# Power in two parts at six layer norms, one power for a double normalisation, and combination weights stacked on 72 partitions in two mixture routers

## The chip, the cores and the metric

One NeuronCore of a Trainium2 chip runs the whole program; the other seven are idle. The metric is device time of one execution in microseconds (us), lower is better. The program is one launch: everything from the inputs in HBM to the output in HBM lies inside it.

## The reference, cut to what matters

A graph network of four layers on 625 nodes with 512 features and 10,000 edges. Each layer adds a graph part and a feed-forward part to the residual `x`, and each part begins with a layer norm over the 512 features of a node:

```
x = x + L0_gnn(layernorm(x));  x = x + L0_ffn(layernorm(x))   # SAGE; causal attention, then softmax mixture of 8 experts
x = x + L1_gnn(layernorm(x));  x = x + L1_ffn(layernorm(x))   # 2 graph-transformer layers; top-2 experts
x = x + L2_gnn(layernorm(x));  x = x + L2_ffn(layernorm(x))   # EGC convolution; 8 experts with top-2 weights
x = x + L3_gnn(layernorm(x));  x = x + L3_ffn(layernorm(x))   # GCN convolution; top-2 experts
```

`layernorm(x) = (x - mean) / sqrt(var + 1e-5)`. `L0_ffn` itself starts with a layer norm of its own, so two normalisations follow each other there. Its mixture, and that of `L2_ffn`, compute every expert for every node and weigh the results:

```
out = sum_e comb[:, e] * (gelu(x @ W1[e] + b1[e]) @ W2[e] + b2[e])
```

with `comb` the softmax of the router's logits (in `L2_ffn` zeroed outside the two largest).

## The kernel before, in words

**Layout.** The residual `X` lies in SBUF as 5 tiles (T) of 125 nodes on 125 partitions (R), 512 features along each. Matmuls contract over features, so a normalised tile set `XN` is transposed by TensorE (PE) in 128x125 pieces into PSUM (L760, `ln_to_feats`) and copied to `XT`, 4 chunks (C) of 128 features by 625 nodes; VectorE (DVE) copies three of the tiles (L1911), ScalarE (ACT) two (L1473). Products that need accuracy are made of two `fp32r` parts, a rounded high part and a low remainder: DVE subtracts to get the lows.

**Order.** Nothing is scheduled by a tool. Each engine has its instruction list written by hand (the five blocks `sync`, `gpsimd`, `tensor`, `scalar`, `vector`), and the lists meet at counting semaphores. `Chain` counts an engine's own operations on a semaphore, and `c.sync()` lets the engine wait for its own last one. `keep(b, n)` (L771) issues n matmuls on constants into a free PSUM bank where PE would otherwise have nothing to do.

**Layer norms.** `ln0` to `ln8` are one pattern: five row statistics (L1922, one per tile), five aggregations to mean and variance (L1930), one small operation `ve = var + eps` on all five columns (L1932), a power of -0.5 on GpSimd (POOL) by `power()` (L641, `rstd`), then five normalisations on DVE (L1958). `ln1` is written out: its statistics alternate with the additions that make `X` (L1996), and it runs the pattern twice on the 5 numbers per node (power, L2458, L2460, L2462, power again as `ln(2)`, L2465) and then normalises once (L2468). At the same time PE and ACT build the causal graph masks (L1266; ACT L1761 and L1764), and PE's transposes of `ln1` wait for these masks too.

**Mixture routers** (r = 0 in layer 0, r = 2 in layer 2). DVE makes `COMB` (125 nodes x 5 tiles x 8 experts; L2062, L2081). PE transposes it to 8 x 625 (L962). ACT copies it as plain fp32 `combT` (L1534) and as rounded high part `combH` (L1540), DVE subtracts to `combL` (L2093). Both halves lie in 128 partition tiles that ACT had zeroed. PE then spreads the weights of each expert over 128 partitions by matmuls with a selector, in halves of 375 and 250 nodes (`HALVES`), high and low (L977, L978):

```
g = 2 * e + i
if g >= 3:
    pe.wait_ge(S("rt_cb"), 2 * E * (r // 2) + g - 2)
pe.matmul(bank[:, (7, 3, 4)[g % 3], 0:n], SEL[:, e], spreadH[:, lo:lo + n], start=True, stop=False)
```

and ACT copies all 16 pieces to `CB` (L1545) from three banks in turn. Before the spread PE runs `soft_first(r, 0)` and `(r, 1)`, the first products of two units (a unit is one expert and one half; 12 matmuls each, L948). `open_sums` (L955) puts `comb . b2` into the five output banks, one fp32 matmul of K=8 each, three of them inside the spread, two in the mixture. The mixture runs over 16 units: PE `soft_first`, ACT gelu (L1563; its first one loads an activation table), DVE times `CB` (L2315), ACT rounding (L1571), DVE low part (L2321), PE `second` (L997).

**GpSimd and SyncE.** POOL's list starts with constants (L598 on). SP issues the loads; `b2` is loaded on 8 partitions.

Of the kernel before, what the change touches and what calls it, by code (L numbers as in the profile page):

```python
# [113 lines left out]
def graph_network(nc, A, out):  # L114
    ctx = ExitStack()
    with ctx:
# [141 lines left out]
        spreadH, spreadL = (rounded("rB", at, N + 1) for at in (0, 632))  # L258
        combH, combL = (x[0:E, 0:N] for x in (spreadH, spreadL))
# [173 lines left out]
        NORMS = 6 + 2 * T + 2 * LAYERS  # L433
        POW = {"ln0": 1, "degr": 2, "bn0": 3, "ln1": 4, "ln2": 5, "q": 6, "k": 6 + T, "ln3": 6 + 2 * T, "lf": NORMS + 1, "ln4": NORMS + 2,
               "ln5": NORMS + 3, "l2": NORMS + 4, "ln6": NORMS + 5, "ln7": NORMS + 6, "bn3": NORMS + 7, "ln8": NORMS + 8}
        LN = [0, 12] + [16 * (k - 1) for k in range(2, 9)]
        RT_ACT = {0: 0, 1: 9, 2: 14, 3: 23}
# [2334 lines left out]
```

## Time and profile before

| | us |
|---|---|
| median of 3 runs | 1692.26 (1690.21 to 1693.14) |
| the profiled execution's own time | 1694.99 |
| span of that profile | 1693.2 |
| PE busy | 1610.8 (95%), 8735 instructions |
| DVE busy | 1231.3 (73%), 2095 |
| ACT busy | 939.7 (55%), 1590 |
| POOL busy | 283.4 (17%), 262 |

Busy times are of the one profiled execution. PE's share contains the filler matmuls of `keep` and stretches in which it ran at half clock, so it isn't the share of useful work. An instruction line of the trace gives its start, its duration (of a group of neighbours: of the whole group, with "xN"), the engine and line, output<-input with partitions x elements, and in brackets the engine's idle time before it and what ended that.

### The profile page before, as it was taken

How to read it: one execution, taken by the hardware profiler on the slowest of the kernel's cores; microseconds unless marked ns; L12 is line 12 of the kernel's file. 1: busy time of each engine (PE TensorE's matmuls, PEld its weight loads, DVE VectorE, ACT ScalarE, POOL GpSimd, SP SyncE). 2: the span in 40 equal slices, each digit the busy share in tenths (PEclk: the TensorE clock that was granted, in tenths of full speed). 3: DMA queues.
4: the chain of work that ended last, by engine and by line, in shares of the span. 5: the costliest groups of instructions: out<-in, count | busy, mean ns of one | idle time of the engine just before them, and what ended most of it. 6: DMA issues, size and time to landing. Idle time of an engine off the chain costs nothing. (4 is left out here: it accounts for less than half of the span.)

```text
span 1693.2 us, 26308 instructions
## 1 busy us (share of the span) xinstructions
PE 1610.8 (95%) x8735; PEld 1252.0 (74%) x8735; DVE 1231.3 (73%) x2095; ACT 939.7 (55%) x1590; POOL 283.4 (17%) x262
## 2 busy tenths in 40 slices
PE   9998999999989998889999999999899999999998
PEld 8886766868866886468778765775588888888886
DVE  8837661464755574779999768353599999999997
ACT  1424464443623462149999653431288788877884
POOL 0014530010210121069000301000280000000003
PEclk9998999999999999989999999999999999999999
DMA  8010000022000002044853240005043529936003
GB/s 335 14 51 1 1 2 13 1 113 75 2 26 13 1 2 100 25 144 160 323 197 106 80 162 0 1 1 223 25 161 145 234 73 384 364 151 242 21 22 97
DMA packets 42176, 173.09 MB, mean 102 GB/s; under 512 B 10187, under 2 KB 10440, under 8 KB 26617
## 3 DMA queue, kind: packets, MB, share of 16 engines
q1 hardware_dynamic: 28678, 153.68, 23.8%
q0 software_dynamic: 8960, 10.29, 2.3%
q10 hardware_dynamic: 4464, 8.13, 1.3%
q8 instruction: 47, 0.77, 0.2%
q14 instruction: 27, 0.22, 0.0%
HBM read 275.47 MB, written 19.25 MB: 174 GB/s over the span
## 5 line engine op out<-in xcount | busy, mean ns | idle before, releaser
L695 POOL DMA_INDIRECT sb_W<-slots_out,sb_slus x20 | 31.5, 1574 | 545.4 <-DMA slots_out<-sb_rC 539.9
L1489 ACT ACTIVATE sb_rF<-sb_rF,sb_nmx 125x625 f32<-125x625 f32 (+4 forms) x120 | 89.5, 746 | 45.0 <-DVE sb_nmx L2011 44.9
L771 PE MATMUL bank<-sb_ones 128*128 128x512 f32 x220 | 102.9, 617 | 8.8 <-DVE sb_rC L2558 6.3
L641 POOL TENSOR_TENSOR sb_rstd<-sb_ve,sb_half 125x5 f32<-125x5 f32 (+1 forms) x17 | 19.1, 1123 | 478.0 <-DVE sb_ve L1932 267.0
L381 DVE TENSOR_TENSOR sb_rA_r<-sb_W,sb_rA_r 128x1024 fp32r<-128x1024 f32 x68 | 83.2, 1224 | 12.2 <-ACT sb_rA_r L1588 12.0
L2011 DVE CUSTOM_DVE_ANT_0 sb_rF<-bank,sb_rG 125x625 f32<-125x625 f32 x80 | 61.5, 807 | 36.1 <-PE bank L863 35.2
L771 PEld LDWEIGHTS bank<-sb_ones 128*128 128x128 f32 x220 | 41.9, 196 | 57.8 <-issue 48.7
L381 DVE TENSOR_TENSOR sb_XT_r<-sb_W,sb_XT_r 128x1024 fp32r<-128x1024 f32 x68 | 83.3, 1225 | 0.0
L381 DVE TENSOR_TENSOR sb_rB_r<-sb_W,sb_rB_r 128x1024 fp32r<-128x1024 f32 x68 | 83.0, 1221 | 0.0
L1588 ACT ACTIVATE sb_rA_r<-sb_W 128x1024 fp32r<-128x1024 f32 x68 | 71.5, 1052 | 20.0 <-DMA sb_W<-in_w_m 15.9
L1623 ACT ACTIVATE sb_rG_r<-bank 128x512 fp32r<-128x512 f32 x51 | 30.6, 600 | 82.3 <-PE bank L1075 82.3
L903 PE MATMUL bank<-sb_rA,sb_rDE 125*64 125x125 f32 x1040 | 69.3, 276 | 4.5 <-DVE sb_rA L2025 4.3
L2315 DVE TENSOR_TENSOR sb_rF<-sb_rF,sb_rDE 128x375 f32<-128x375 f32 (+1 forms) x32 | 15.4, 486 | 79.7 <-ACT sb_rF L1563 79.7
L875 PE MATMUL bank<-sb_ident,sb_rF 125*125 125x125 f32 x520 | 70.1, 279 | 3.0 <-DVE sb_nmx L2011 3.0
L1588 ACT ACTIVATE sb_XT_r<-sb_W 128x1024 fp32r<-128x1024 f32 x68 | 71.7, 1054 | 0.0
L1588 ACT ACTIVATE sb_rG_r<-sb_W 128x1024 fp32r<-128x1024 f32 x68 | 71.6, 1053 | 0.0
L1588 ACT ACTIVATE sb_rB_r<-sb_W 128x1024 fp32r<-128x1024 f32 x68 | 71.3, 1049 | 0.2 <-PE bank L1053 0.2
L903 PEld LDWEIGHTS bank<-sb_rA,sb_rDE 125*64 125x64 f32 x1040 | 54.9, 136 | 20.7 <-DVE sb_rA L2025 13.1
L875 PEld LDWEIGHTS bank<-sb_ident,sb_rF 125*125 125x125 f32 x520 | 61.5, 189 | 9.0 <-issue 6.8
L381 DVE TENSOR_TENSOR sb_AT_r<-sb_W,sb_rG_r 128x1024 fp32r<-128x1024 f32 x51 | 62.0, 1216 | 0.0
L2025 DVE COPY sb_rA<-bank 125x500 f32<-125x500 f32 (+3 forms) x60 | 37.6, 627 | 31.0 <-PE bank L875 30.9
L1049 PE MATMUL bank<-sb_XT_r,sb_rC_r 128*128 128x512 f32 x136 | 59.4, 437 | 0.0
(534 smaller groups left out, 4839.1 us busy)
## 6 DMA issues: line engine op xcount, KB each, us to landing
sb_W<-in_w_m SPq DMA_DIRECT2D x204, 1024.0 KB
sb_rDE<-in_w_m SPq DMA_DIRECT2D x17, 1024.0 KB
sb_rC<-slots_in SPq DMA_DIRECT2D x33, 256.0 KB, 2.7
sb_W<-in_w_g SPq DMA_DIRECT2D x8, 1024.0 KB, 4.9
slots_out<-sb_rC ACTq DMA_DIRECT2D x31, 256.0 KB, 2.0
slots_in<-sb_rC SPq DMA_DIRECT2D x1, 4608.0 KB, 24.7
sb_W<-in_w_a SPq DMA_DIRECT2D x4, 1024.0 KB, 17.9
sb_W<-in_w_m SPq DMA_DIRECT2D x2, 2048.0 KB, 16.4
```

The lines of the kernel that those rows point to most:

```text
L381: eng.tensor_tensor(lo, src[:, HALF * h:HALF * (h + 1)], hi.bitcast(F32), ALU.subtract).then_inc(split(r, p, h, b, "lo")[0], 1)
L641: pool.tensor_tensor(dst, src, half8[0:src.shape[0], :].broadcast_to([src.shape[0], k]), ALU.pow).then_inc(S("pow"), 1)
L695: pool.indirect_dma_start(out=G[r][k][:, t], out_offset=None, in_=YS[0:P * KEPT[r]], in_offset=bass.IndirectOffsetOnAxis(ap=slus[:, k, t:t ...
L771: pe.matmul(bank[:, b, :], ones[:], ones[:, 0:1].broadcast_to([P, D]), start=True, stop=True)
L875: return pe.transpose(bank[0:R, b, at:at + R], SM[:, (2 * p + a) % 4, kb * R:(kb + 1) * R], ident[0:R, 0:R])
L903: mm = pe.matmul(bank[a * DH:(a + 1) * DH, 6 + g % 2, p % 2 * R:(p % 2 + 1) * R], V[:, kb, h + a, :], PT[:, p % 2, 8 + a if kb == 4 else 4 ...
L1049: pe.matmul(dst, high[2 * h + k], w_hi[:, k], start=(opens and h == 0 and k == 0), stop=False)
L1489: act.activation(SM[:, s % 4, 0:kn], SM[:, s % 4, 0:kn], ACT.Exp, scale=-1.0, bias=nmx[:, s:s + 1], accum_out=dens[:, s:s + 1]).then_inc(S ...
L1588: act.activation(half(r, p, h)[0], part(PLACE[r][p])[:, HALF * h:HALF * (h + 1)], ACT.Copy).then_inc(split(r, p, h, b, "hi")[0], 1)
L1623: act.activation(hTh[:, j % 2], src, ACT.Copy).then_inc(S("b_ht"), 1)
L2011: dve.tensor_tensor_reduce(out=SM[:, s % 4, 0:kn], in0=scores, in1=mask(t), scale=-1.0, scalar=3e38, op0=ALU.add, op1=ALU.min, accum_out=n ...
L2025: dve.tensor_copy(PT[:, p % 2, 4:4 + nb, :], pt).then_inc(S("at_pt"), 1)
```

## The change: what it does

**1. Power in two parts.** For ln1 and ln3 to ln8 the aggregation, `ve` and power of tiles 0 to 2 are issued after the third row statistic, those of tiles 3 and 4 after the fifth; the normalisation of tile 0 waits for the first power, that of tile 3 for the second.

```diff
                 c(dve.bn_stats(st[0:R, t], src(t)))
-            moments(c)
+                if t == 2:
+                    moments(c, 0, 3, twice)
+            moments(c, 3, T, twice)
...
         def normalise(c, k, src):
-            dve.wait_ge(S("pow"), POW[f"ln{k}"])
             for t in range(T):
+                if t in (0, 3):
+                    dve.wait_ge(S("pow"), POW[f"ln{k}"] - (1 if t == 0 and k > 0 else 0))
...
         def ln(k):
-            power(rstd3[:] if k == 2 else rstd[0:R, :], ve[0:R, :], T, S("ln_vec"), LN[k] + 11 if k != 2 else LN[1] + 14)
+            if k > 0:
+                power(rstd[0:R, 0:3], ve[0:R, 0:3], 3, S("ln_vec"), LN[k] + FIRST)
+                power(rstd[0:R, 3:T], ve[0:R, 3:T], T - 3, S("ln_vec"), LN[k] + STATS)
```

**2. One power for the double normalisation of ln1.** `ve = var * (1 + EPS) + EPS * EPS`; the second power and four small DVE operations go.

```diff
-            dve.wait_ge(S("pow"), POW["ln1"])
-            c(dve.tensor_tensor(rstd2[:], rstd[0:R, :], rstd[0:R, :], ALU.mult))
...
-            dve.wait_ge(S("pow"), POW["ln2"])
-            c(dve.tensor_tensor(rstd2[:], rstd[0:R, :], rstd3[:], ALU.mult))
...
+                    c(dve.tensor_scalar(ve[0:R, a:b], mv[0:R, a:b, 1], 1 + EPS, EPS * EPS, ALU.mult, ALU.add))
```

DVE's list at `ln1`, where `rstd` names the small scale tiles, `mv` mean and variance; before:

```order
278 L1922 BN_STATS sb_st<-sb_X 125x6
279 L1996 TENSOR_TENSOR sb_X<-bank,sb_X 125x512
280 L1922 BN_STATS sb_st<-sb_X 125x6
281 L1930 BN_AGGR sb_mv<-sb_st 125x2 x5
282 L1932 TENSOR_SCALAR sb_ve<-sb_mv 125x5
283 L2458 TENSOR_TENSOR sb_rstd<-sb_rstd 125x5
284 L2460 TENSOR_TENSOR sb_rstd<-sb_rstd,sb_mv 125x5
285 L2462 TENSOR_SCALAR sb_ve<-sb_rstd 125x5
286 L2465 TENSOR_TENSOR sb_rstd<-sb_rstd 125x5
287 L2468 TENSOR_SCALAR sb_XN<-sb_X,sb_mv,sb_rstd 125x512 x5
```

The same place after the change:

```order
276 L1936 BN_STATS sb_st<-sb_X 125x6
277 L1946 BN_AGGR sb_mv<-sb_st 125x2 x3
278 L1949 TENSOR_SCALAR sb_ve<-sb_mv 125x3
279 L2016 TENSOR_TENSOR sb_X<-bank,sb_X 125x512
280 L1936 BN_STATS sb_st<-sb_X 125x6
281 L2016 TENSOR_TENSOR sb_X<-bank,sb_X 125x512
282 L1936 BN_STATS sb_st<-sb_X 125x6
283 L1946 BN_AGGR sb_mv<-sb_st 125x2 x2
284 L1949 TENSOR_SCALAR sb_ve<-sb_mv 125x2
285 L1978 TENSOR_SCALAR sb_XN<-sb_X,sb_mv,sb_rstd 125x512 x5
```

Three aggregations and a `ve` moved ahead of the last two additions to `X`; the four small operations between `ve` and the normalisation are gone.

**3. Combination weights stacked (routers 0 and 2).** DVE writes the weights three times side by side (`COMB3`, columns 0, 32 and 64; a MEMSET of 125x480 ahead), so that one set of transposes gives 72 partitions. ACT copies those once, rounded (72x500, 72x125); DVE subtracts on partitions 32 to 39 only, so the stack holds high, low, high. One matmul of K=72 spreads both parts. `b2` is loaded at partitions 0, 32 and 64 (three DMAs for one, twice; SP waits for a POOL memset of 72x512), ACT rounds it (72x512), DVE makes its low part at 64 (8x512), and `open_sums` is one `fp32r` matmul of the stack with it. ACT's two zero fills of 128x626 and its four copies of 8 partitions go. The 128x250 pieces of `CB` are copied by DVE (banks 4, 2), ACT keeps the 128x375 ones (banks 7, 3). One more AFFINE_SELECT on POOL makes the selector's rows 32 to 39.

```diff
             soft_first(r, 0)
-            soft_first(r, 1)
-            pe.wait_ge(S("rt_act"), RT_ACT[r] + 9)
-            pe.wait_ge(S("comb_low"), r + 2)
+            pe.wait_ge(S("rt_act"), RT_ACT[r] + 6)
+            pe.wait_ge(S("comb_low"), 3 * (r // 2) + 3)
             for e in range(E):
+                if e == 4:
+                    soft_first(r, 1)
                 for i, (lo, hi) in enumerate(HALVES):
-                    g = 2 * e + i
-                    if g >= 3:
-                        pe.wait_ge(S("rt_cb"), 2 * E * (r // 2) + g - 2)
+                    if e >= 2:
+                        pe.wait_ge(S(("rt_cb", "rt_cbv")[i]), E * (r // 2) + e - 1)
...
+                    pe.matmul(bank[:, CB_BANK[i][e % 2], 0:n], SEL[0:STACK, e], stack[:, lo:lo + n],
+                              start=True, stop=True).then_inc(S("rt_spread"), 1)
+                if e in (2, 5):
+                    open_sums(e // 3, e // 3 + 1)
...
             for u in range(2, UNITS + 2):
-                if u < 4:
-                    open_sums(u + 1, u + 2)
+                if u == 2:
+                    open_sums(2, T)
```

PE's list in router 0, from the last matmul of `soft_first` (written on the buffers `XN_r`, `XT_r`, `rA_r`) into the spread (on `rB_r` and `SEL`); before:

```order
402 L948 MATMUL bank<-sb_XN_r_2500_53,sb_rA_r_512_71 128x250
403 L948 MATMUL bank<-sb_XT_r_2500_51,sb_W_r_512_119 128x250
404 L977 MATMUL bank<-sb_rB_r_626_75,sb_SEL 128x376
405 L978 MATMUL bank<-sb_rB_r_626_76,sb_SEL 128x376
406 L977 MATMUL bank<-sb_rB_r_626_75,sb_SEL 128x250
407 L978 MATMUL bank<-sb_rB_r_626_76,sb_SEL 128x250
```

After the change (L971 is `open_sums`, L964 `soft_first`):

```order
396 L993 MATMUL bank<-sb_rB_r_626_75,sb_SEL 128x376
397 L993 MATMUL bank<-sb_rB_r_626_75,sb_SEL 128x250
398 L971 MATMUL bank<-sb_W_r_512_76,sb_rB_r_626_75 125x512
399 L993 MATMUL bank<-sb_rB_r_626_75,sb_SEL 128x376
400 L993 MATMUL bank<-sb_rB_r_626_75,sb_SEL 128x250
401 L964 MATMUL bank<-sb_XT_r_2500_51,sb_rA_r_512_71 128x250
```

Each piece is one matmul where it was two, and the second unit's first products, which stood ahead of the spread, stand in its middle. DVE's list at the same router gains the copies and moves one `soft_low` (L2342, the low part of an expert's weights) ahead of them:

```order
460 L2085 TENSOR_TENSOR sb_W<-sb_EX,sb_red 125x15x8
461 L2122 TENSOR_TENSOR sb_W_r_512_76<-sb_b,sb_W_r_512_76 8x512
462 L2342 TENSOR_TENSOR sb_W_r_512_120<-sb_W,sb_rA_r_512_72 128x512
463 L2126 TENSOR_TENSOR sb_rB_r_626_75<-bank,sb_rB_r_626_75 8x500
464 L2126 TENSOR_TENSOR sb_rB_r_626_75<-bank,sb_rB_r_626_75 8x125
465 L2131 COPY sb_rDE<-bank 128x250 x8
466 L2342 TENSOR_TENSOR sb_W_r_512_121<-sb_W,sb_rA_r_512_73 128x512
```

Where two `soft_low` followed the two lows directly before, the second now stands behind eight copies.

**4.** Some semaphores are merged (`g_bq` into `g_qk_vec`, `msk_done` and `rows_pool` into `pool_done`, `next_rows` into `rows_off`), with the counts of their waits adjusted. The instructions between them are the same. The two top-2 routers (r = 1, 3) and all edge code compute as before.

## Rows read from the trace of the kernel before

**Rows 1.** The page's first part: busy time, share and instructions.

```profile
PE 1610.8 (95%) x8735; PEld 1252.0 (74%) x8735; DVE 1231.3 (73%) x2095; ACT 939.7 (55%) x1590; POOL 283.4 (17%) x262
```

**Rows 2.** Windows: busy time of PE, PEld, DVE, ACT, POOL, then clock, DMA, GB/s.

```profile
1083.00:1136.00 53.00, 52.07 (x275) 43.84 (x274) 24.89 (x48) 18.15 (x40) 0.00 (x0) 1.00 0.00 1
...
283.00:286.00 3.00, 3.00 (x12) 3.00 (x11) 1.92 (x4) 1.05 (x4) 0.00 (x0) 0.50 0.00 0
```

**Rows 3.** The timeline of ln3, 350 to 366: start, duration, engine, line, operation.

```profile
354.96 3.07 DVE L1922 BATCH_NORM_STATS2 sb_st<-sb_X 125x6 f32<-125x512 f32 x5
...
358.07 0.44 DVE L1930 BATCH_NORM_AGGREGATE sb_mv<-sb_st 125x2 f32<-125x6 f32 x5
...
358.55 0.17 DVE L1932 TENSOR_SCALAR sb_ve<-sb_mv 125x5 f32<-125x5 f32 x1
358.79 1.17 POOL L641 TENSOR_TENSOR sb_rstd<-sb_ve,sb_half 125x5 f32<-125x5 f32 x1 [104.38 <-DVE sb_ve L1932]
360.00 2.37 DVE L1958 TENSOR_SCALAR sb_XN<-sb_X,sb_mv,sb_rstd 125x512 f32<-125x512 f32 x5 [1.28 <-POOL sb_rstd L641]
...
360.60 2.48 PE L760 MATMUL bank<-sb_ident,sb_XN 125*128 125x125 f32 x20 [1.36 <-DVE sb_XN L1958]
...
362.28 1.84 DVE L1911 COPY sb_XT<-bank 128x500 f32<-128x500 f32 x3
```

**Rows 4.** Groups of POOL by form: busy, mean ns, idle before and releaser.

```profile
L641 POOL TENSOR_TENSOR sb_rstd<-sb_ve,sb_half 128x4 f32<-128x4 f32 x6 | 6.1, 1010 | 145.8 <-DVE sb_ve L1974 145.8
```

**Rows 5.** Powers beside DVE work: timeline, then three powers' min/median/max ns.

```profile
39.06 1.32 POOL L641 TENSOR_TENSOR sb_rstd<-sb_ve,sb_half 125x5 f32<-125x5 f32 x1 [26.97 <-DVE sb_ve L1932]
...
171.21 2.28 DVE L2483 TENSOR_TENSOR sb_W_r<-sb_W,sb_XN_r 128x2048 fp32r<-128x2048 f32 x1
...
L641 POOL TENSOR_TENSOR sb_ssr<-sb_ss,sb_half x3: 2023/2059/2820, 170.1 to 175.0; 125x8 f32<-125x8 f32 x3
```

**Rows 6.** The timeline of ln7.

```profile
1139.01 3.97 PE L760 MATMUL bank<-sb_ident,sb_XN 125*128 125x125 f32 x20 [3.69 <-DVE sb_XN L1958]
```

**Rows 7.** The timeline around ln1, 116 to 142.

```profile
131.75 2.99 PE L1266 MATMUL bank<-sb_ident,sb_AT 125*125 125x125 f32 x25 [0.98 <-DVE sb_X L1996]
...
138.59 0.43 ACT L1764 ACTIVATE sb_rG<-bank,sb_below 125x125 f32<-125x125 f32 x1
139.07 2.35 PE L760 MATMUL bank<-sb_ident,sb_XN 125*128 125x125 f32 x20 [1.74 <-ACT sb_rG L1764]
```

**Rows 8.** The timeline of router 2 and the mixture's start, 1061 to 1085.

```profile
1061.89 0.69 PE L962 MATMUL bank<-sb_ident,sb_COMB 125*8 125x125 f32 x5 [1.55 <-DVE sb_COMB L2081]
...
1063.73 0.25 ACT L1540 ACTIVATE sb_rB_r<-bank 8x125 fp32r<-8x125 f32 x1
...
1064.51 0.28 PE L948 MATMUL bank<-sb_rC_r,sb_rA_r 128*128 128x250 f32 x1
...
1065.91 0.34 PE L977 MATMUL bank<-sb_rB_r,sb_SEL 128*128 128x376 f32 x1
...
1066.45 1.94 ACT L1545 ACTIVATE sb_rDE<-bank 128x375 f32<-128x375 f32 x5 [2.47 <-PE bank L978]
...
1067.80 1.12 PE L955 MATMUL bank<-sb_b,sb_rF 8*125 8x512 f32 x2
...
1075.70 1.28 ACT L1563 ACT_TABLE_LOAD   x1
...
1079.50 0.47 PE L997 MATMUL bank<-sb_rA_r,sb_rF_r 128*125 128x512 f32 x1 [0.37 <-DVE sb_rB_r L2321]
...
1084.18 0.50 PE L997 MATMUL bank<-sb_rA_r,sb_rF_r 128*125 128x512 f32 x1
```

**Rows 9.** The timeline of router 0, the same two places.

```profile
285.94 0.41 PE L948 MATMUL bank<-sb_XT_r,sb_rA_r 128*128 128x250 f32 x1
...
301.09 0.47 PE L997 MATMUL bank<-sb_rA_r,sb_rF_r 128*125 128x512 f32 x1 [0.37 <-DVE sb_rB_r L2321]
```

**Rows 10.** POOL's timeline at the program's start.

```profile
0.91 0.53 POOL L599 MEMSET sb_rC<- 128x512 f32 x1
```

More of the change, by code:

```diff
@@ L44 @@
 H = 8
+STACK = 72
 DH = D // H
@@ L257, in graph_network @@
         SELf = W[:, 16384:16384 + E * P].rearrange("p (e n) -> p e n", e=E)
-        spreadH, spreadL = (rounded("rB", at, N + 1) for at in (0, 632))
-        combH, combL = (x[0:E, 0:N] for x in (spreadH, spreadL))
+        stack = rounded("rB", 0, N + 1)[0:STACK]
+        COMB3 = W[0:R, 16896:16896 + T * 3 * 32].rearrange("p (t k e) -> p t k e", t=T, k=3)
+        b2r = rounded("W", 16384, D)[0:STACK]
         CB = rDE[:, 0:E * N].rearrange("p (e n) -> p e n", e=E)
@@ L429, in fifths @@
             return min(p, H // 2) if causal else H // 2 + base(PAIRS) - PAIRS + p
[L433 to L437, printed above, removed]
+        POWERS = (["ln0", "degr", "bn0", "ln1a", "ln1"] + ["q"] * T + ["k"] * T + ["ln3a", "ln3"] + ["layers"] * (2 * LAYERS)
+                  + ["lf", "ln4a", "ln4", "ln5a", "ln5", "l2", "ln6a", "ln6", "ln7a", "ln7", "bn3", "ln8a", "ln8"])
+        POW = {name: POWERS.index(name) + 1 for name in POWERS}
+        FIRST, STATS = 7, 12
+        LN = [0, STATS, None] + [12 + 17 * (k - 2) for k in range(3, 9)]
+        RT_ACT = {0: 0, 1: 6, 2: 11, 3: 17}
         LAST_BN = 16 + 32 * LAYERS
-        ROUTER_OPS = (6, 24, 21, 24)
+        ROUTER_OPS = (7, 24, 22, 24)
         SLOT_OPS = 17 + 2 * T
@@ L773, in ln_to_feats @@
             def ln_to_feats(k, behind=None):
-                to_feats(XN, S("tr_full"), S("ln_vec"), LN[k] + 11 if k != 2 else LN[1] + 15, 1, behind)
+                to_feats(XN, S("tr_full"), S("ln_vec"), LN[k] + STATS, 1, behind)
             def streamed(dst, gains, xt, i, done):
@@ L954, in open_sums @@
                 for t in range(a, b):
-                    pe.matmul(bank[0:R, t, :], combT[:, t * R:(t + 1) * R], b2[:], start=True, stop=False, skip_group_check=True)
+                    pe.matmul(bank[0:R, t, :], stack[:, t * R:(t + 1) * R], b2r, start=True, stop=False, skip_group_check=True)
             def router(r):
@@ L1026, in second_biases @@
                     for t in range(a, b):
-                        pe.matmul(bank[0:R, (3, 2, 4, 5, 7)[t], :], combT[:, t * R:(t + 1) * R], b2[:], start=True, stop=True).then_inc(S("b2_full"), 1)
+                        pe.matmul(bank[0:R, (3, 2, 4, 5, 7)[t], :], combT[:, t * R:(t + 1) * R], b2, start=True, stop=True).then_inc(S("b2_full"), 1)
                     return
@@ L1525, in router @@
             def router(r):
-                act.wait_ge(S("rt_vec"), ROUTED[r] + 3)
+                act.wait_ge(S("rt_vec"), ROUTED[r] + (4 if r in (0, 2) else 3))
                 act.activation(EX[:], LG[:], ACT.Exp).then_inc(S("rt_act"), 1)
-                if r in (0, 2):
-                    for x in (spreadH, spreadL):
-                        act.activation(x, ones[:, 0:1].broadcast_to([P, N + 1]), ACT.Copy, scale=0.0).then_inc(S("rt_act"), 1)
                 if r == 3:
                     return
-                act.wait_ge(S("rt_pe"), 4 * r + 4)
@@ L1915, in feats, with stats_rows @@
                 copy_feats(dst, S("tr_full"), S("tr_v"), T * k, scale)
-            def stats_rows(c, src, before=None):
+            def stats_rows(c, src, before=None, twice=False):
                 for t in range(T):
@@ L2045, in router @@
                 c = Chain(dve, S("rt_vec"), ROUTED[r])
+                if r in (0, 2):
+                    c(dve.memset(COMB3, 0.0))
                 dve.wait_ge(S("rt_pe"), 4 * r + 3)
```

152 lines of the change are left out of this document (86 added, 66 removed).

## The prediction

> **What bounds the kernel now.** I read the busy shares first, then the windows by stage, then the timeline where the change acts. TensorE is busy 95% of the span [rows 1], but that says little here: filler matmuls and half-clock stretches count as busy. The windows tell more. In the mixture of layer 2 PE is busy 52.07 of 53 us at full clock [rows 2], so what the change does to ACT and DVE there is worth nothing. Around the layer norms and in the routers PE waits. In ln3 the last row statistic ends at 354.96 + 3.07 = 358.03 and the normalisation starts at 360.00, behind five aggregations, one small operation and a power of 1.17; PE's transposes start on the first normalised tile, with 1.36 idle [rows 3]. In router 2 PE starts the spread at 1065.91, ACT copies until the table load at 1075.70, and the first `second` starts at 1079.50, 3.8 later, by way of gelu, product and rounding [rows 8]. These serial stretches are what the change can shorten. Nothing else moves the end.
>
> **ln3 to ln8, power in two parts.** The wait from the last statistic to the normalisation is 1.97 now. Afterwards two parts stand in its place. Ahead of statistics 4 and 5: three aggregations at 0.44 / 5 = 0.09, one `ve` of 0.17, and some 0.04 between dependent steps: about 0.55. Behind the last: two aggregations, one `ve`: about 0.45. Gain 1.97 - 1.00 = 0.97 each [rows 3]. It needs both powers in time. The first has 1.2 (two statistics at 3.07 / 5 = 0.61) plus 0.45. The second must end before the normalisation of tile 3, which is three at 2.37 / 5 = 0.47, so 1.4, after its `ve` [rows 3]. The powers of four and five columns take 1.01 and 1.17 [rows 3, 4], a slope of 0.16, so I estimate 0.85 for three columns and 0.69 for two, at most 1.01. Both fit. Next comes DVE itself: normalisations and copies fill it [rows 3], so everything behind moves up whole. Filler matmuls ahead of the transposes don't bind, since PE still idles 1.36 there. Six sites (ln3, ln4, ln5, ln6, ln7, ln8): **5.8 us**.
>
> Here a row and a rule part. The second power now runs beside normalisations, DVE operations from SBUF to SBUF. A power beside such operations at 39.06 took 1.32, not 1.17; powers of eight columns near the large subtraction at 171.21 took 2.02 to 2.82 [rows 5]. I read this as a delay of 0.15 to 0.8 on POOL's side, and the slack of the second power is 1.4 - 0.7 = 0.7, so I take no loss. The Trainium skill, page "SBUF — State Buffer", section "Who interferes with whom", says that VectorE and GpSimd share one port pair as an exclusive lock, held for the whole instruction. By that rule the two would take turns, and each site would lose up to a power; the rows agree in kind (a power is late) but not in that size at 39.06.
>
> **ln1.** Its saved power and four small operations look like the largest item, some 3 us of DVE waiting. But PE's transposes there start at 139.07, released by ACT's mask work, which ends at 138.59 + 0.43; PE's mask transposes that feed it start at 131.75, released by the last addition to `X` [rows 7]. The three aggregations and `ve` now stand ahead of the last two additions and push this whole chain by 0.55. So the single power saves nothing on the path, and the split costs **0.55 us**. Without masks as cover the item would be worth 3.
>
> **Routers: ahead of the spread.** The second unit's 12 matmuls leave the place ahead of the spread, so it can start where the first of them starts now, 1064.51 [rows 8]. Is the stack ready? ACT has two copies instead of four, which end at 1063.73 + 0.25 now, and DVE's lows take 0.86 after; with two copies fewer that is before 1064.6. The wider product (120 for 40 columns) and the wider transposes cost 0.1 to 0.2. The spread starts at S = 1064.7.
>
> **The spread.** Now it lasts from 1065.91 to 1075.70, 9.8: 16 copies on one engine, at 1.94 / 5 = 0.39 each, plus three fp32 bias matmuls in two passes which hold PE 1.12 each, as at 1067.80, and so starve ACT [rows 8]. Afterwards: 0.54 until the first copy (as 1065.91 to 1066.45), eight copies on ACT of 0.39 to 0.48 (bank handshake), taken as 0.43, so 3.4, and `soft_first(r, 1)` in the middle, 1065.91 - 1064.51 = 1.4, which both copy engines sit out: 5.3 [rows 8]. DVE's 250-column copies take less than the 0.61 of a 500-column one [rows 3], so DVE keeps pace. The bias matmuls become single fp32r ones; the nearest row is the 0.34 of a rounded matmul. Behind the spread comes the same 3.8. So `second` starts at 1064.7 + 5.3 + 3.8 = 1073.8 instead of 1079.5: 5.7. The `soft_low` now behind eight copies holds back PE's `soft_first(r, 2)` by some 0.6, a new wait, but it lies beside the table load and gelu chain, so it costs nothing; without that cover it would cost 0.6. In the PE-bound mixture the bias matmul ahead of 1084.18 goes, 1.12 by its kind less 0.07 of overlap with its neighbour: 1.05 [rows 8]. Router 2: **6.8 us**.
>
> Router 0 starts its spread where 285.94 stands, S = 286.1; `second` follows at 295.2 instead of 301.09: 5.9 [rows 9], plus 1.05: **6.9 us**. The clock there is at half in 283 to 286 [rows 2] before and presumably after.
>
> **Priced at nothing.** Two more b2 DMAs on SP, twice, wanted only in a router. The POOL memset of 72x512 (at most 0.53, as one of 128x512 [rows 10]) delays the iota by less than the input edges take to arrive. The selector's AFFINE_SELECT runs while POOL idles. DVE's COMB3 MEMSET stands ahead of a wait for logits. Merged semaphores count what their waits needed anyway. If one of these covers fails, it costs at most some 0.5 us.
>
> **Sum.** 5.8 - 0.55 + 6.8 + 6.9 = 19.0. The profiled execution took 1694.99 and would take 1676.0; it is 2.7 above the median of the runs, 1692.26, which gives **1673.3 us**. The measurement can tell about 0.2% (3.4 us) from no change; this is 1.1%.
>
> **Rivals.**
> *A, as summed*, 1669 to 1677: 0.58.
> *B, powers and normalisations exclude each other.* At six sites 0.8 (one power of two columns with its handshake) is lost: gain 14.2, **1678.1**. For it: the 2.82 power in rows 5, and the skill's rule above. Against: the 1.32. Chance 0.16.
> *C, the routers pay less.* Two banks per engine, not three per ACT, may hand over slower (0.2 for each of 8 copies: 1.6 per router), or TensorE's clock falls in the spread, where PE has half its former work; a half-clock stretch like 283 to 286 costs half its length, 1.5. Together up to 3 in each router, gain 13 to 16: **1677.5**. Chance 0.14.
> *D, more.* ln7's transposes run at half clock after 3.69 of idle, 3.97 instead of 2.48 [rows 6]; with the idle at 2.7 they may not, which gives 1.5 more, and ACT's handshake at 0.39 gives 0.3 per router: 1671.2; other half-clock stretches may vanish too: **1670** and below. Chance 0.08.
> *E, slower.* The lighter spread leaves the clock at 1.2 GHz as the mixture begins and it stays there. The mixture is 53 us of PE-bound work [rows 2]; all of it at half clock would add 53, **1726**. It decides from 19 us of full-clock work done at half. Against: the half-clock stretch at 283 in a fully busy PE was over after 3.5 us. Chance 0.02.
> *F, nothing arrives*: the shortened stretches are waited out elsewhere, by loads of weights for example, **1692**. Against: each norm's first matmul follows DVE's copies. Chance 0.02.
>
> **Range.** The low end takes A's good side with D's items, the high end B with part of C: 1667.5 to 1680.5. The signs: faster 0.96, within 0.2% 0.02, slower 0.02.
>
> **What would show it.** At each of the six norms, last statistic to first normalisation about 0.5, the second power near 0.7 and no gap ahead of the fourth normalisation (a gap: B). At ln1, PE's transposes still released by ACT, 0.5 later relative to the first addition. In both routers, 9.1 from the first spread matmul to the first `second`, and PE clock 1.00 in that window (otherwise C). The prediction is wrong if any of the six sites shows DVE waiting after the split, if the spread lasts over 7 us, or if the difference lies in a stage that isn't named here.

## The result, and the profile after

| | before | after |
|---|---|---|
| median of the runs | 1692.62 | 1676.32 (1674.75 to 1678.03, 4 runs) |
| ratio | | 0.9897, 95% interval 0.988 to 0.9913 |
| span of the profiled execution | 1693.2 | 1676.3 |

16.3 us faster, 1.0%. The forecast was 1673.3 with a range of 1667.5 to 1680.5; the sum said 19.0, so about 2.7 are missing. Each experiment below is compared by its ratio to runs of the kernel before that were made with it, since single runs of one kernel scatter by 3 to 9 us.

The page after, its first part; beside [rows 1] PE is 11 us less busy, DVE 10 more, ACT 8 less:

```profile
PE 1599.8 (95%) x8693; PEld 1247.8 (74%) x8693; DVE 1241.1 (74%) x2118; ACT 932.0 (56%) x1568; POOL 290.5 (17%) x270
```

**A norm after.** The timeline of ln3, against [rows 3]:

```profile
351.09 1.88 DVE L1936 BATCH_NORM_STATS2 sb_st<-sb_X 125x6 f32<-125x512 f32 x3
353.01 0.31 DVE L1946 BATCH_NORM_AGGREGATE sb_mv<-sb_st 125x2 f32<-125x6 f32 x3
353.35 0.17 DVE L1951 TENSOR_SCALAR sb_ve<-sb_mv 125x3 f32<-125x3 f32 x1
353.43 1.28 DVE L1936 BATCH_NORM_STATS2 sb_st<-sb_X 125x6 f32<-125x512 f32 x2
353.60 0.85 POOL L652 TENSOR_TENSOR sb_rstd<-sb_ve,sb_half 125x3 f32<-125x3 f32 x1 [98.69 <-DVE sb_ve L1951]
354.75 0.25 DVE L1946 BATCH_NORM_AGGREGATE sb_mv<-sb_st 125x2 f32<-125x6 f32 x2
355.03 0.17 DVE L1951 TENSOR_SCALAR sb_ve<-sb_mv 125x2 f32<-125x2 f32 x1
355.11 2.37 DVE L1978 TENSOR_SCALAR sb_XN<-sb_X,sb_mv,sb_rstd 125x512 f32<-125x512 f32 x5
355.28 0.92 POOL L652 TENSOR_TENSOR sb_rstd<-sb_ve,sb_half 125x2 f32<-125x2 f32 x1 [0.83 <-DVE sb_ve L1951]
```

The last statistic ends at 353.43 + 1.28 = 354.71, the normalisation starts at 355.11: 0.40 where it was 1.97. It runs without a gap although the second power ends at 356.20, an estimated 0.3 ahead of the fourth normalisation (three of the five in 2.37 are 1.4). At all six sites this wait is 0.4. The two halves of the trade can be seen when the same DVE operations of both traces are laid side by side: at every site the statistics of tile 3 come 0.54 later relative to those ahead, and the normalisation 1.56 earlier relative to the last statistic. Net 1.02, forecast 0.97. The first power isn't the same everywhere. At ln4 (and ln6, 1.22) it took far more than the 0.85 of ln3, beside an addition of DVE:

```profile
698.70 0.74 DVE L2620 SCALAR_TENSOR_TENSOR sb_X<-sb_XN,sb_rstd,sb_X 125x512 f32<-125x512 f32 x1
698.87 1.28 POOL L652 TENSOR_TENSOR sb_rstd<-sb_ve,sb_half 125x3 f32<-125x3 f32 x1 [6.18 <-DVE sb_ve L1951]
```

It ends at 700.15 and the normalisation begins at 701.03, so this costs nothing either.

**ln1 after**, against [rows 7]:

```profile
132.41 2.99 PE L1282 MATMUL bank<-sb_ident,sb_AT 125*125 125x125 f32 x25 [1.54 <-DVE sb_X L2016]
...
133.47 2.37 DVE L1978 TENSOR_SCALAR sb_XN<-sb_X,sb_mv,sb_rstd 125x512 f32<-125x512 f32 x5
...
139.72 2.35 PE L774 MATMUL bank<-sb_ident,sb_XN 125*128 125x125 f32 x20 [1.73 <-ACT sb_rG L1778]
```

The normalisation begins 3.05 earlier than before and ends at 135.84; PE's transposes begin 0.65 later, at 139.72, released by ACT's masks as before. Of the 0.65, 0.1 was already there at the stage's beginning; 0.55 is the delay of the last additions. The saved power gave nothing: before, the normalisations ended at 136.52 + 2.37 = 138.89, just ahead of the 139.07 at which PE started on the masks' signal.

**Router 2 after**, against [rows 8]:

```profile
1053.93 0.70 PE L978 MATMUL bank<-sb_ident,sb_W 125*72 125x125 f32 x5 [1.62 <-DVE sb_W L2108]
...
1056.55 0.73 PE L993 MATMUL bank<-sb_rB_r,sb_SEL 72*128 72x376 f32 x4
1056.92 0.86 ACT L1559 ACTIVATE sb_rDE<-bank 128x375 f32<-128x375 f32 x2 [1.51 <-PE bank L993]
1057.03 0.74 DVE L2131 COPY sb_rDE<-bank 128x250 f32<-128x250 f32 x2 [0.72 <-PE bank L993]
...
1062.04 1.28 ACT L1577 ACT_TABLE_LOAD   x1
1062.10 0.69 DVE L2342 TENSOR_TENSOR sb_W_r<-sb_W,sb_rA_r 128x512 fp32r<-128x512 f32 x1
...
1062.93 0.41 PE L964 MATMUL bank<-sb_rC_r,sb_rA_r 128*128 128x376 f32 x1 [1.33 <-DVE sb_W_r L2342]
...
1065.08 0.85 PE L971 MATMUL bank<-sb_W_r,sb_rB_r 72*125 72x512 f32 x3
...
1065.87 0.47 PE L1013 MATMUL bank<-sb_rA_r,sb_rF_r 128*125 128x512 f32 x1
```

From the transposes to the spread 2.62 (4.01 before), from the spread to the first `second` 9.32 (13.59); forecast for the latter were 9.1. The transposes to 72 partitions take 0.70, those to 8 took 0.69: the wider stack costs PE nothing. The new wait for the third weight's low part is there, and longer than forecast: 1.33.

**Router 0** is the place that fell short. Transposes to first `second`, in the traces:

| | router 0 | router 2 | first to last `second` |
|---|---|---|---|
| before | 19.13 | 17.61 | 51.72 |
| after | 14.27 | 11.93 | 50.51, 50.49 |
| gain | 4.86 | 5.68 | 1.2 each |

Its clock, in windows of after (busy time of PE, PEld, DVE, ACT, POOL, then the clock), beside the 3.4 at half clock before [rows 2]:

```profile
283.20:286.60 3.40, 2.44 (x10) 2.37 (x11) 2.44 (x6) 1.31 (x4) 0.00 (x0) 0.50 0.00 0
286.60:290.00 3.40, 3.40 (x13) 3.21 (x11) 0.76 (x3) 0.48 (x1) 0.00 (x0) 0.50 0.03 5
515.40:518.70 3.30, 3.30 (x5) 1.24 (x5) 2.01 (x11) 0.48 (x1) 1.01 (x1) 0.50 0.01 5
```

and, of before, the place that answers to the last of these:

```profile
520.10:523.50 3.40, 3.40 (x8) 1.53 (x9) 2.10 (x11) 0.39 (x1) 1.01 (x1) 1.00 0.08 30
```

At that place, in the first graph-transformer layer, the two programs do the same. PE idles 2.5 in both (2.51 until 520.01 before, 2.50 until 515.13 after) and then runs fillers. Before, the clock stayed at 2.4 GHz; after, it was at 1.2, and everything behind came 1.69 later. The stretches at half clock sum to 44.2 us in the trace of before and 54.4 after. (These sums leave out a last stretch that begins after PE's last matmul.) That gave the theory for the runs: the steps are as forecast, and the missing part is TensorE's clock, which falls in other places from one execution to the next.

### The profile page after: what moved, and what is told of

Its sections match the earlier page's. It is cut to its first block, busy times and chain, and to the rows that moved or that the text cites. A ratio compares the mean times of both kernels' runs of the same rounds, so it can differ in the third digit from the quotient of the medians.

```text
span 1676.3 us, 26239 instructions
## 1 busy us (share of the span) xinstructions
PE 1599.8 (95%) x8693; PEld 1247.8 (74%) x8693; DVE 1241.1 (74%) x2118; ACT 932.0 (56%) x1568; POOL 290.5 (17%) x270
## 4 chain that ended last, share of the span: by engine, by line
PE 77%; DVE 13%; issue 3%; DMA 2%; ACT 2%; POOL 1%; SPq 0%; DVEq 0%; ACTq 0%; POOLq 0%
PE bank L1065 10%; PE bank L1069 10%; PE bank L1066 10%; PE bank L829 5%; PE bank L917 4%; PE bank L889 4%; PE bank L964 3%; PE bank L877 3%; PE bank L1013 3%; PE bank L1189 3%; PE bank L1297 3%; PE bank L848 2%; PE bank L1091 2%; PE bank L1271 2%; PE bank L840 2%
## 5 line engine op out<-in xcount | busy, mean ns | idle before, releaser
L785 PE MATMUL bank<-sb_ones 128*128 128x512 f32 x220 | 106.4, 634 | 8.8 <-DVE sb_rC L2584 6.3
L652 POOL TENSOR_TENSOR sb_rstd<-sb_ve,sb_half 125x3 f32<-125x3 f32 (+3 forms) x23 | 22.9, 998 | 458.3 <-DVE sb_ve L1951 239.9
L917 PEld LDWEIGHTS bank<-sb_rA,sb_rDE 125*64 125x64 f32 x1040 | 55.0, 137 | 20.7 <-DVE sb_rA L2045 13.1
L1065 PE MATMUL bank<-sb_rA_r,sb_rC_r 128*128 128x512 f32 x136 | 53.7, 395 | 5.5 <-ACT sb_rC_r L1616 2.9
```

The costliest lines, as they stand in the source:

```text
L785: pe.matmul(bank[:, b, :], ones[:], ones[:, 0:1].broadcast_to([P, D]), start=True, stop=True)
L917: mm = pe.matmul(bank[a * DH:(a + 1) * DH, 6 + g % 2, p % 2 * R:(p % 2 + 1) * R], V[:, kb, h + a, :], PT[:, p % 2, 8 + a if kb == 4 else 4 ...
L1065: pe.matmul(dst, high[2 * h + k], w_hi[:, k], start=(opens and h == 0 and k == 0), stop=False)
```

## The experiments

**Control: the changed kernel once more.**

> The changed kernel once more, as a control. Theory (clock): the 2.7 us that are missing from the predicted 19.0 are TensorE at half clock for longer (54.4 us of the span against 44.2 before), and where the clock falls differs from one execution to the next; then this trace shows half-clock stretches at partly other places, and the time is 1674 to 1678. Rival (routers): the missing part is fixed, in the routers; then the stretches are where they were, and the time 1676.3 within 0.5.

Measured: 1675.42 (1672.96 to 1677.06), ratio 0.9899 (0.9884 to 0.9914), the profile's span 1671.2: 5.1 shorter than that of the first profile, from the same program. Its half-clock stretches sum to 47.6, 6.8 less, and some of them lie elsewhere; the one near 515 is where it was:

```profile
283.70:287.10 3.40, 3.29 (x21) 2.98 (x21) 2.43 (x6) 1.23 (x4) 0.00 (x0) 1.00 0.00 0
292.80:296.20 3.40, 3.40 (x12) 3.40 (x12) 1.44 (x3) 1.64 (x4) 0.00 (x0) 0.50 0.00 0
514.80:518.10 3.30, 3.30 (x5) 1.24 (x5) 1.86 (x8) 1.38 (x2) 1.01 (x1) 0.50 0.01 2
```

In router 0 the clock fell behind the spread and not ahead of it (transposes to `second` 13.33 instead of 14.27); the fall near 679, which before and after both have, is missing. The norm steps (0.54 and 1.56) and router 2 (11.89) are the same to 0.1. The fixed rival falls: the steps are fixed, the clock is not. The 5.1 can be placed. When ln5's normalisations start (974.66 and 969.62) the control is already 5.04 ahead, and up to there it has 10.2 less at half clock (37.4 against 47.6), worth at most 5.1; 0.32 was there at ln1's first addition to `X`. Behind ln5 the control has a stretch more, at 1170, and loses no time by it. So a half-clock stretch costs up to half its length, and sometimes nothing.

**The two halves alone.** The powers only: the kernel before with the parts 1, 2 and 4 of the change, routers untouched.

> The kernel before with only the powers in two parts and the single power of ln1; routers as before. Theory: 6 x 1.0 less 0.55 at ln1, so 5.4 faster than before: 1687.2. Rival (powers and normalisations take turns): 1 or less gained, 1691.5. Rival (routers short): 5.4 gained here, and the shortfall all in the other half.

Measured: 1685.93, ratio 0.996 (0.9944 to 0.9976), so 6.8 faster (4 to 9.5). In its trace the six sites show 0.54 and 1.56 again and the routers 19.14 and 17.60, as before.

The routers only:

```diff
-                    power(rstd[0:R, 0:3], ve[0:R, 0:3], 3, S("ln_vec"), LN[k] + FIRST)
-                    power(rstd[0:R, 3:T], ve[0:R, 3:T], T - 3, S("ln_vec"), LN[k] + STATS)
...
+                power(rstd[0:R, :], ve[0:R, :], T, S("ln_vec"), LN[k] + 11)
...
-                    if t == 2:
-                        moments(c, 0, 3, twice)
-                moments(c, 3, T, twice)
+                moments(c, 0, T, twice)
```

> The changed kernel with one power of five columns per norm again (ln1 keeps its single power), so the routers' part alone. Theory: 13.1 faster than before (5.6 + 1.2 in router 2, the like in router 0 less what the clock takes): 1679.5, 0.55 of which comes from ln1's additions no longer being held up. Rival (routers short): 10 to 11 faster, 1682.

Measured: 1686.19, ratio 0.9958 (0.9944 to 0.9972), 7.1 faster by the ratio: outside both expectations, and half of what the steps say. Yet its profile, the fastest of its runs, had a span of 1680.4, 12.8 below before, with router 2 at 11.94 and router 0, with one fall ahead of its spread and one behind it, at 14.70. So it was run again.

> The routers' part alone once more, since its runs were 6.8 faster than before but its trace, the fastest of them, 12.8. Theory (the scatter is TensorE's clock, another pattern of half-clock stretches in each execution): the median lies nearer to 1681.5 this time, at least 9 faster than before, and the trace has each router step as it was, 5.6 + 1.2 in router 2. Rival (the part gives only 7 by itself): 1686 again.

Measured: 1681.86, ratio 0.9933 (0.9914 to 0.9952), 11.3 faster; router 2 11.93, router 0 13.16. The first median was 4.3 higher for the same file. Between them the two intervals reach from 4.7 to 14.5, and the 13.1 of the steps lies in the second. With the powers' 6.8 (4 to 9.5) they make 14 to 18; both together gave 17. The halves add up within that scatter, and nothing finer can be said from run times of this kernel: the steps in the traces are the better measure.

**Does the split pay because powers and normalisations overlap?** Every first normalisation waits for both powers:

```diff
-                    if t in (0, 3):
-                        dve.wait_ge(S("pow"), POW[f"ln{k}"] - (1 if t == 0 and k > 0 else 0))
+                    if t == 0:
+                        dve.wait_ge(S("pow"), POW[f"ln{k}"])
```

> The changed kernel, but every norm's first normalisation waits for the second power too. Theory (powers and normalisations overlap, so the split pays): each of ln3 to ln8 starts normalising about 0.85 later, +5 us in all, 1681; and the second power, now with no DVE operation beside it, takes 0.69 where it takes 0.92 beside one. ln1 stays as it is. Rival (they take turns already): +1 us or less.

Measured: 1679.76, ratio 0.9925 (0.9912 to 0.9938), so 4.4 slower than the changed kernel's 0.9899 (5.5 expected from 6 x 0.91, and the two intervals touch). Its ln3:

```profile
353.90 0.70 POOL L652 TENSOR_TENSOR sb_rstd<-sb_ve,sb_half 125x2 f32<-125x2 f32 x1 [0.82 <-DVE sb_ve L1951]
354.64 2.37 DVE L1978 TENSOR_SCALAR sb_XN<-sb_X,sb_mv,sb_rstd 125x512 f32<-125x512 f32 x5 [0.81 <-POOL sb_rstd L652]
```

The wait from last statistic to normalisation is 1.30 at all sites, 0.91 more. A power of two columns takes 0.70 alone and 0.92 beside normalisations; five normalisations take 2.37 in both. So POOL gives way by 0.22 and DVE by nothing, and the slack takes the 0.22. Rival B, which asked for 0.8 lost per site, falls.

What remains open is how POOL loses the 0.22. When the power starts at 355.28, the first normalisation, begun at 355.11, has an estimated 0.3 to run (five in 2.37), so one wait for its end isn't excluded. A five-column power beside normalisations, in the run of ln1's longer power below, lost the same 0.22 (1.39 and 1.16):

```profile
L660 POOL TENSOR_TENSOR sb_rstd<-sb_ve,sb_half x2: 1161/1276/1392, 133.2 to 134.6; 125x5 f32<-125x5 f32 x2
```

At ln4 above, beside an operation that ran another 0.57, the loss was 0.43. Beside row statistics alone (ln3's first power, 0.85) there was none. So the loss goes with what DVE was doing when the power started and not with the power's length. DVE is the side that never waited, though its next normalisations began inside the power.

The Trainium skill ("SBUF — State Buffer", "Who interferes with whom") states that where VectorE, in a two-port mode, and GpSimd contend, whoever issues first gets the shared ports for its whole instruction and the other fully blocks. POOL's losses fit a wait for DVE's instruction; that DVE would wait for POOL's whole 0.92 is what the trace does not show. No row tells in which mode the normalisations ran.

**ln1's aggregations behind the last addition:**

```diff
...
+                    if twice and t == 4:
+                        moments(c, 0, 3, twice)
                     c(dve.bn_stats(st[0:R, t], src(t)))
-                    if t == 2:
+                    if t == 2 and not twice:
```

> The changed kernel with ln1's first three aggregations and their ve moved behind the last addition to X. Theory: the mask chain of PE and ACT starts 0.55 earlier and the transposes of ln1 with it: 0.55 faster than the changed kernel, PE's first mask transpose at 131.85 instead of 132.41. Rival (hidden): no change, since the transposes would then wait for the normalisation.

Measured: 1673.74, ratio 0.9884 (0.9868 to 0.9899). In the trace the mask transposes start at 131.29 and the transposes of ln1 at 138.61, where after had 132.41 and 139.72. The execution was already 0.57 ahead at the stage's first addition to `X` (125.27 against 125.84), and the transposes are 1.11 earlier, so 0.54 is the edit's, where 0.55 was expected: all of the loss comes back. The time's 1.7 against the control is inside the scatter.

**ln1's power made longer**, by two more powers of five columns ahead of its second one:

```diff
+                    if k == 1:
+                        pool.wait_ge(S("ln_vec"), LN[k] + STATS)
+                        for spare_rows in (rstd2, rstd3):
+                            pool.tensor_tensor(spare_rows[:], ve[0:R, :], half8[0:R, :].broadcast_to([R, T]), ALU.pow)
```

> The changed kernel with two more powers of five columns on POOL ahead of ln1's second power, their results unused: ln1's normalisations of tiles 3 and 4 start some 2.4 later. Theory (ln1's power is hidden behind ACT's masks, which release PE's transposes 4 us after the normalisations end): PE's transposes start where they did, 139.7, and no time changes. Rival: 2.4 later.

Measured: 1673.80, ratio 0.9886 (0.9863 to 0.9909). Its trace:

```profile
133.25 2.52 POOL L660 TENSOR_TENSOR sb_rstd<-sb_ve,sb_half 125x5 f32<-125x5 f32 x2 [2.27 <-DVE sb_ve L1953]
...
136.47 1.00 DVE L1982 TENSOR_SCALAR sb_XN<-sb_X,sb_mv,sb_rstd 125x512 f32<-125x512 f32 x2 [1.95 <-POOL sb_rstd L652]
...
139.32 2.35 PE L778 MATMUL bank<-sb_ident,sb_XN 125*128 125x125 f32 x20 [1.73 <-ACT sb_rG L1782]
```

DVE waits 1.95 for the power and PE's transposes still start on ACT's mask (this execution was 0.4 ahead at the first addition, 125.44 against 125.84). What hides 2.5 added here hid the 3 that were saved.

**The spread.** All 16 copies on ACT:

```diff
-                    lo, hi = HALVES[0]
-                    act.wait_ge(S("rt_spread"), 2 * E * (r // 2) + 2 * e + 1)
...
+                    for i, (lo, hi) in enumerate(HALVES):
+                        act.wait_ge(S("rt_spread"), 2 * E * (r // 2) + 2 * e + i + 1)
...
-                        dve.tensor_copy(CB[:, e, lo:hi], bank[:, (4, 2)[e % 2], 0:hi - lo]).then_inc(S("rt_cbv"), 1)
```

> The changed kernel with all 16 CB copies on ACT. Theory (the copies pace the spread): 8 copies of 128x250 at 0.3 to 0.37 on ACT lengthen each spread by about 2.0, so +4 us, 1680; half of the router's gain is the second copy engine. Rival (PE's matmuls and the removed fp32 bias pairs pace it): under +1 us.

Measured: 1676.99, ratio 0.9901 (0.9887 to 0.9916), no difference that the runs can tell; in the trace router 2 takes 12.97 instead of 11.93:

```profile
1055.95 2.70 ACT L1559 ACTIVATE sb_rDE<-bank 128x375 f32<-128x375 f32 x8 [1.50 <-PE bank L993]
```

Eight copies of both sizes take 2.70, 0.34 each, and two such groups make a spread. The second copy engine is worth 1.0 per router, half of what was expected. So of the 4.3 gained behind the spread's start, 3.2 come from the rest: single matmuls, single-pass biases, and the second unit's work between the copies. No run takes the first two apart.

The second unit's first products back ahead of the spread:

```diff
                 soft_first(r, 0)
+                soft_first(r, 1)
...
-                    if e == 4:
-                        soft_first(r, 1)
```

> The changed kernel with the second unit's first products back ahead of the spread. Theory (the spread is a serial chain of copies and PE work, and this work is on it wherever it stands): the first second() comes within 0.3 of where it was in both routers, 1676. Rival (the move itself gave the gain): 1.4 later per router, 1678.5.

Measured: 1678.21, ratio 0.9916 (0.9895 to 0.9936). Router 2 took 14.52, but this execution had the clock at half for 6.8 us inside it, so it can't be set against 11.93. Router 0 can be compared with the control's, since in both the clock fell at 292 to 296: 13.62 against 13.33. That is 0.3, for the theory; one pair of numbers is thin, and the run times lean the other way: 2.9 slower than the changed kernel by the ratios, which is what the rival said, in overlapping intervals. The move's worth stays open between 0.3 and 1.4 per router.

The third weight's low part ahead of DVE's copies:

```diff
+                    soft_low(r, 2)
                     for e in range(E):
                         lo, hi = HALVES[1]
...
-                soft_low(r, 2)
```

> The changed kernel with the low part of the third expert weight made ahead of the eight DVE copies, not behind them. Theory: PE's wait of 1.33 at the mixture's start goes, and the first second() starts 0.0 to 0.15 earlier per router, since gelu, product and rounding end at the same time; no change that can be measured. Rival (this wait is part of the shortfall): second() 0.6 or more earlier per router.

Measured: 1675.39, ratio 0.9901 (0.9888 to 0.9914). PE's wait ahead of the mixture falls from 1.33 to 0.56, and instead it waits at the first `second`:

```profile
1059.05 0.41 PE L964 MATMUL bank<-sb_rC_r,sb_rA_r 128*128 128x376 f32 x1 [0.56 <-ACT sb_rDE L1559]
...
1062.75 0.47 PE L1013 MATMUL bank<-sb_rA_r,sb_rF_r 128*125 128x512 f32 x1 [0.71 <-DVE sb_rB_r L2358]
```

Transposes to `second`: 11.92 against 11.93. The new wait costs nothing; it was hidden behind the gelu chain, as forecast. In router 0, 14.29 against 14.27.

**Fillers against the falls.** With ln1 late, more filler matmuls where PE idled ahead of half-clock stretches:

```diff
+                keep(0, 4 if r == 0 else 3)
...
+                pe.wait_ge(S("h_done"), layer * 16 + 17)
+                keep(0, 5)
                 pe.wait_ge(S("h_done"), layer * 16 + 24)
...
+            keep(7, 5)
             ln_to_feats(7)
...
-            keep(7, 6)
+            keep(7, 9)
```

> The changed kernel with ln1's aggregations late and with filler matmuls where PE idled ahead of half-clock stretches: 4 and 3 ahead of the routers' transposes, 5 behind the first residual of each graph-transformer layer, 5 ahead of ln7, 3 more ahead of ln8. Theory (the clock falls behind idle stretches of PE): the falls at 283, 515, 679, 1123 go, each worth about 1.7, so 4 to 7 us on top of the 0.55: 1669. Rival (the falls come regardless of idle time, at random): the fillers give nothing, 1675, and half-clock time stays 45 to 55.

Measured: 1678.72, ratio 0.991 (0.9897 to 0.9924): 4.4 slower by the ratios than with ln1 late alone, with 40.8 at half clock. The twelve traces without added fillers have 40.8 to 54.4 (the lowest is that of the powers alone), so the sum doesn't show that the clock did what was hoped. That the fillers were too long is clear. Router 0's transposes, with ln1 late alone and then with 4 fillers ahead of them; up to there both have the same half-clock stretches:

```profile
282.93 0.70 PE L978 MATMUL bank<-sb_ident,sb_W 125*72 125x125 f32 x5 [1.89 <-DVE sb_W L2087]
```

```profile
280.93 3.71 PE L785 MATMUL bank<-sb_ones 128*128 128x512 f32 x8
284.49 0.70 PE L979 MATMUL bank<-sb_ident,sb_W 125*72 125x125 f32 x5
```

3.71 of fillers went into an idle stretch of 1.89, and the router begins 1.56 later. In ln8's place, first of the changed kernel, with 6 fillers, then of this one, with 9:

```profile
1176.60 5.34 PE L785 MATMUL bank<-sb_ones 128*128 128x512 f32 x12
...
1183.36 2.47 PE L774 MATMUL bank<-sb_ident,sb_XN 125*128 125x125 f32 x20 [1.43 <-DVE sb_XN L1978]
```

```profile
1177.74 8.30 PE L785 MATMUL bank<-sb_ones 128*128 128x512 f32 x18
1185.88 2.30 PE L774 MATMUL bank<-sb_ident,sb_XN 125*128 125x125 f32 x20
```

Six fillers are 12 records: each is two passes, together 5.34 / 6 = 0.89. Three more are an estimated 2.7 us, put into an idle stretch of 1.43. Counted from the stage's first addition to `X` (1175.12 and 1174.97) the transposes come 2.7 later, but here part of it is a half-clock stretch at 1175.08 that delayed the fillers' start. The same fillers, halved in number or fewer, again with ln1 late, and with the third weight's low part first:

> The version meant to be best: ln1's aggregations late, the third weight's low part first, and fillers of the right length. A filler matmul is fp32 and takes PE 0.87 (two passes), not 0.43; so now 2 in router 0, 1 in router 2, 2 behind the first residual of each graph-transformer layer, 2 ahead of ln7, 1 more ahead of ln8. Theory (the clock falls behind idle stretches of PE, and the fillers before were too long): no site is delayed, the falls near 515, 679 and 1123 go, 1671 or less. Rival (falls come at random): 1674, as with ln1 late alone.

Measured: 1668.73 (1668.23 to 1674.51), ratio 0.9868 (0.9842 to 0.9894), the fastest of all kernels here: 22 below before. Its span was 1666.5, its half-clock time 34.0. Router 0 and the place at 515:

```profile
282.20:285.60 3.40, 3.35 (x22) 3.06 (x21) 3.15 (x6) 1.16 (x4) 0.00 (x0) 1.00 0.00 0
285.60:294.00 8.40, 7.15 (x41) 6.07 (x41) 4.28 (x11) 5.86 (x12) 0.00 (x0) 1.00 0.01 2
510.90:518.00 7.10, 7.10 (x19) 3.45 (x20) 2.92 (x13) 1.71 (x2) 1.01 (x1) 1.00 0.02 8
```

All at full clock, and transposes to `second` is 11.97 in router 0 and 11.96 in router 2: without a fall the two routers are one. The falls near 283, 515, 679 and 1123 are gone; those at ln1, behind the causal attention and in the block loop's start, where no filler was put, are still there, and so are two around ln8 (1165 and 1189), where one was added. How much is the fillers' doing? In the twelve traces without added fillers the fall near 515 comes in 5 and that near 679 in 3, so that they are missing here shows little. The fall ahead of router 0's spread comes in 10, and the one at ln7's transposes (1123 in after, 1139.6 in before) in all twelve; it is missing in both traces with fillers. That one, by this count, the fillers removed.

By the ratios this kernel is 5 faster than the changed one. Its interval overlaps the changed kernel's (0.988 to 0.9913 and 0.9884 to 0.9914) by 0.0014 at most, and one of its four runs was at 1674.51, so that is likely and not tight. Against the kernel with ln1 late alone (0.9868 to 0.9899) it is 2.7, inside the scatter: what the fillers alone are worth isn't shown.

## Why the prediction was right, and which term was off

- **The six norms**: forecast 5.8, in the trace 6 x 1.02 = 6.1. Both halves of the trade are in all traces that have the split, and the wait for both powers put most of it back (0.91 per site).
- **ln1**: forecast a loss of 0.55 and nothing from the saved power. Shown: 0.55 in the trace, 0.54 of it back when the aggregations go late, and 2.5 us of added power vanish behind the masks.
- **Powers beside normalisations**: forecast no loss. Shown: 0.22 on POOL, inside the slack, and up to 0.43 for a first power. The slack was thin: of 0.7 forecast some 0.3 were left, since the power begins 0.17 behind the first normalisation and takes 0.22 more.
- **Router 2**: forecast 5.7 + 1.05, measured 5.68 + 1.2. The parts were less exact than the sum: the spread to `second` is 9.32 instead of 9.1, and the wait for the low part 1.33 instead of 0.6, both without effect or nearly.
- **Router 0**: forecast 5.9 + 1.05, measured 4.86 + 1.2. This is the term that was mis-sized. Its step was "the clock there is at half in 283 to 286 before and presumably after": after, half clock lasted from 283.2 to 290.0. With the clock full it takes 11.97. Of the 1.0 that is missing 0.65 lie ahead of the spread (from the transposes 4.79, forecast 286.1 - 281.96 = 4.14) and the rest behind it (9.47, forecast 9.1).
- **Elsewhere**: the steps add to 6.1 - 0.55 + 6.9 + 6.1 = 18.5, the spans differ by 16.9. The remaining 1.6 are 0.1 ahead of ln1 and a balance of larger parts, in stages that the change touches at most by a merged semaphore. The prediction had named a difference in such a stage as a sign of being wrong. By size it came up three times. Lost: 1.55 between ln1's transposes and router 0's (142.89 before, 144.44 after), where the stretch that begins at 252 lasts 10.2 instead of 6.8; 1.69 near 515. Gained: 1.85 in layer 1's experts, from ln4's first normalisation to ln5's (276.50 before, 273.63 after, less the 1.02 of ln5's own step), 1.4 of it where before has a fall, at 753.9, and after has none (both have 13.6 at half clock in that stage, but not at the same places); the rest of the 1.85 isn't placed. The rows of before, then of after:

```profile
258.94:262.34 3.40, 3.40 (x15) 2.59 (x14) 0.00 (x0) 1.17 (x4) 0.00 (x0) 1.00 0.00 0
753.90:757.30 3.40, 3.40 (x11) 2.61 (x10) 3.40 (x4) 2.62 (x3) 3.40 (x2) 0.50 0.29 120
```

```profile
259.26:262.66 3.40, 3.40 (x8) 2.04 (x7) 0.00 (x0) 0.61 (x2) 0.00 (x0) 0.50 0.00 0
750.00:753.40 3.40, 3.40 (x17) 2.82 (x18) 3.40 (x4) 3.40 (x7) 3.40 (x2) 1.00 0.39 161
```

- **Rival C** had the clock in mind, and by the prediction's own sign (full clock from the first spread matmul to the first `second`) it came up in router 0: in after the first 1.0 of these 9.47 was at half clock, in the control 3.4 of 10.73. In router 2 both had the full clock, but the traces of the wait for both powers and of ln1 late had 3.4 at half clock between the spread and `second` too (from 1060.0 and 1059.1), and took 13.4 instead of 11.9. So C's clock part is real, and a router that it hits in full pays 1.4 (10.73 against 9.32). Its other part, a slower handover between banks, is at most the 0.2 between 9.32 and the 9.1 forecast.

How much of the 2.7 between the medians is the clock, and how much scatter of four runs (the control's median is 0.9 lower), these runs can't separate.

The steps' forecast was sound; that the time came out within 3.0 of it is in part luck. The forecast assumed that the changed kernel's pattern of falls would cost what the old one's did. The first profile of it had 10.2 us more half-clock time, the control 3.4 more, and the falls outside the changed places happened to cancel down to 1.6. The range held because its high end had room for this.

## What to carry to other kernels

Before pricing a saved operation, look at who releases the consumer: ln1's saved power looked like the largest single item and was worth nothing, while moving four short operations ahead of two additions cost half a microsecond. A long serial step of few columns can be split so that its first part runs beside the work that produces the rest, and what that is worth is the wait in the trace less the operations that now stand ahead. Where gains of a few microseconds are judged in a program whose clock falls in other places from one execution to the next, lay the two traces side by side step by step, and take several executions: two medians of the same file differed by 4.3 us here. Before a fall that is missing is put down to an edit, count in how many traces without the edit it is missing too. And measure a filler's length in the trace before choosing their number.

## What the runs showed of the hardware

- The same 2.5 us of PE idle at the same place was followed by the 2.4 GHz level in one execution and by 1.2 GHz in another (520.10 in before, 515.40 in after); in the control a fall that two other traces have was missing. PE ran without a break ahead of the return at 290.0 (286.60 to 290.00 above). Most falls stand behind a stretch in which PE had idled in part, but not all; in after, one stands behind 3.4 us of busy PE:

```profile
733.75:737.15 3.40, 3.40 (x11) 1.65 (x10) 3.28 (x7) 0.00 (x0) 2.94 (x4) 1.00 0.52 136
737.15:740.55 3.40, 3.40 (x9) 2.22 (x7) 3.33 (x12) 0.00 (x0) 1.06 (x5) 0.50 0.82 246
```

- Half-clock time was 40.8 to 54.4 us in twelve traces without added fillers, and 40.8 and 34.0 in the two with them.
- A power on GpSimd beside normalisations on VectorE: 0.92 instead of 0.70 for two columns, 1.39 instead of 1.16 for five, VectorE unchanged at 2.37 for five. Beside an addition with two inputs in SBUF (ln4), three columns took 1.28 instead of 0.85.
- Transposing 72 columns instead of 8 costs PE the same (0.70 and 0.69 for five), and a product written three times as wide costs DVE 0.08 more (0.28 for 120 columns, 0.20 for 40).
